# Token preparation of each image inside the last steps of the Mamba pipeline, in place of a block of its own

## The chip, the cores and the metric

One core of a Trainium2 chip runs the whole program in one launch. The metric is the device time of that launch in microseconds (us). All arithmetic is in f32; sort keys and indices are 32-bit integers. TensorE does the matrix products and the 128x128 transposes, VectorE and ScalarE the elementwise work, GpSimd (POOL) additions and the indirect transfers, and SyncE (SP) issues nearly all other transfers. Each engine works through its own queue in program order and waits on semaphores.

## The reference, cut to what matters

x has 16 images of 128 channels and 32x32 = 1024 places.

```
x1  = x + conv_branch(layer_norm_over_channels(x))     # two Mamba layers and a residual path r
t   = x1 as tokens [16, 1024, 128]                     # one token per place
n   = layer_norm(t)                                    # over the 128 channels, eps 1e-5
h   = n @ W_gat                                        # 16 columns: 4 heads x 4 experts
a_src, a_dst = sum over experts of h * att_src, h * att_dst      # 4 + 4 columns
score = graph attention over 524288 edges and 16384 loops (gather h and a_src of each edge's source)
out = t + mixture of 4 experts, top 2 by score, of n   # GELU MLPs, 128 -> 256 -> 128
```

Token preparation is what this document calls the lines from x1 to a_src and a_dst: x1 = v + x (v is the output of the second Mamba layer with its residual, x the input), x1 turned so that tokens lie on the partitions, the norm, the turn back (the experts want channels on the partitions), and the product with the 128x24 matrix [W_gat, W_gat*att_src, W_gat*att_dst], whose 24 columns are one row of the table that the edges gather from. x1, the normalised tokens of all images (64 KB a partition) and the table (16384 rows of 96 bytes) are kept.

## The kernel before, in words

The program is a chain of blocks; all engines meet at the end of each. The first block is the Mamba pipeline with the sort of the edges laid between its instructions. A prologue over 16 images comes first, then a loop of `STEPS` = 82 steps, t = 0 to 81. In step t below `NJ` = 64, TensorE projects one tile of 128 rows of a group of four images (`in_part`, L587), first half of the output (z = 0) and gate (z = 1). ScalarE moves it out and VectorE convolves (`conv`, L930). Nine steps behind (`SCAN_AT`), TensorE gives the step size (`dt_part`, L619), ScalarE makes softplus (`softplus`, L764 to L767, with an activation table load), then the decays of the tile before it (`decay`, L774), then `logarithm` (L781); VectorE adds (`step_size`, L942) and, one step later, scans (`scan`, L952 to L975). Behind a whole group, the output product goes in units of six chunks a step (`out_part`, L604; a chunk is 128 rows of the output weight, 512 KB, loaded by SP into one of four buffers, each load waiting for the chunk that had the buffer). Each step takes them two at a time in three places of TensorE's queue. An image is complete after eight chunks; VectorE norms it (`norm_first`, L981, and `norm_second`, L992 to L1001, in places fixed by dictionaries of steps), ScalarE applies Silu (L807, `put_out`) and in the second layer the result v goes to DRAM (L498). The last scan belongs to step 73, the output chunks of the last four images to steps 74 to 79, their norms and Silu to steps 75 to 80.

The sort's last comparison (L899, L900) is in step 58. Step `search` = 66 begins the search for the places where each partition's part of the edges starts: VectorE counts rows (L1070 to L1074), POOL gathers three sets of 128 rows of 4096 keys (L550, 6 MB), and VectorE compares and sums them at the end of step 68 (L1078, L1081). Two more small steps (lengths by DRAM and back, L527 and L529, and the number of rounds, L1091 to L1098) follow at 69 and 71.

The second block is token preparation. SP loads v and x of an image (L1150), POOL adds them (L1186), SP stores the sum (L1169), TensorE turns it (`turn`, L1196, eight 128x128 transposes), VectorE takes statistics (L1229, L1232), ScalarE the root (L1267), VectorE scale and shift (L1238, L1239), ScalarE normalises (L1272), TensorE turns back (L1216), ScalarE copies to `tok_t` (L1279), TensorE multiplies with the 128x24 matrix (`project`, L1205), VectorE copies the rows (L1247) and SP stores them (L1155). The tiles in PSUM that TensorE writes are double, except the one of the turn back, and each engine runs about an image ahead of the next.

The third block gathers table rows for the edges, 1280 indirect transfers on POOL (L1449), with the experts' products beside them; it needs the whole table. It starts with constants and memsets on POOL (L1419 to L1436), after which VectorE makes the addresses (L1577 to L1580) and POOL fetches the first keys (L1440). A last block mixes.

The order of work on each engine is written out by hand in the loop over t; nothing is planned by costs.

Of the kernel before, what the change touches and what calls it, by code (L numbers as in the profile page):

```python
# [12 lines left out]
P = 128  # L13
# [101 lines left out]
STEPS = KC * (NI - 1) + OUT_AT + (4 * KC - 1) // UNITS + 3  # L115
# [50 lines left out]
def program(nc, a, stop=99):  # L166
# [12 lines left out]
    with ctx:  # L179
# [27 lines left out]
        rounds_i = sb("rounds_i", [1, 1], I32)  # L207

# [19 lines left out]
        with ExitStack() as st, nc.Block() as block:  # L228
            w = [{k: a[f"m{m}_{k}"] for k in ("WinT", "convw", "convb", "WxT", "WdtT", "bdt", "Alog", "D", "WoutT")}
                 for m in (1, 2)]  # L230
            keys = [sb(f"keys{n}", [P, KF], F32, st) for n in range(2)]
            xT = sb("xT", [P, 2, KC, QW], F32, st)
# [36 lines left out]
            len_max = sb("len_max", [1, 1], F32, st)  # L269
            slots_i = sb("slots_i", [1, 1], I32, st)  # L270
# [73 lines left out]
            s_v = first_sem("s_v")  # L344
            s_vst = [first_sem("s_vst0"), first_sem("s_vst1")]
# [17 lines left out]
            search = KC * (NI - 1) + KC + 2  # L363
            spare = keys[1 - keys_in(len(plan))]
            row_of = [xT[:, x].rearrange("p k n -> p (k n)") for x in range(2)] + [spare[:]]
            firsts = w_in[:, 0, 0, :]
            before = w_in[:, 0, 1:4, :]
            len_row = w_in[0:1, 1, 0:3, :]
            len_f = w_in[0:1, 1, 3:5, :]
            pad = w_in[0:1, 0, 4, :].bitcast(I32)  # L370

            @block.sync
            def _(sp):
# [36 lines left out]
                def load_image(b):  # L410
                    if b < B:
                        if b >= 2:
                            sp.wait_ge(s_pt, b - 1)
                        sp.dma_start(xin[b % 2], x_in[b]).then_inc(s_px[b % 2], 16)

# [42 lines left out]
                for t in range(STEPS):  # L458
# [37 lines left out]
                    elif n is not None:  # L496
# [13 lines left out]
                    if t == search - 1:  # L510
# [3 lines left out]
                        sp.wait_ge(s_cmp, done_at[-1])  # L514
                        last = keys[keys_in(len(plan))]
                        sp.dma_start(sorted_d[0:NE, :].rearrange("(p c) o -> p (c o)", p=P),
                                     last[:].bitcast(I32)).then_inc(s_stored, 16)
                        with nc.allow_non_contiguous_dma(reason="one key of a row"):
                            sp.dma_start(first_d[:, :], last[:, 0:1]).then_inc(s_first, 16)
                        sp.wait_ge(s_first, 16)  # L520
                        sp.wait_ge(s_mz, NJ)
                        sp.dma_start(firsts, first_d[:, :].rearrange("p o -> o p").partition_broadcast(P)
                                     .rearrange("p o n -> p (o n)")).then_inc(s_first, 16)
                    if t == search + 3:
                        sp.wait_ge(s_len, 1)
                        with nc.allow_non_contiguous_dma(reason="three places of a row"):
                            sp.dma_start(len_d[:, :].rearrange("o p -> p o"), ends_f[:]).then_inc(s_lend, 16)  # L527
                        sp.wait_ge(s_lend, 16)
                        sp.dma_start(len_row, len_d[:, :].rearrange("(x o) p -> x o p", x=1)).then_inc(s_lend, 16)  # L529
                for x in range(2):  # L530
                    sp.wait_ge(s_vst[x], 16 * B // 2)
                sp.wait_ge(s_lend, 32)

            @block.gpsimd
            def _(g):
# [9 lines left out]
                g.wait_ge(s_mz, NJ)  # L545
# [3 lines left out]
                for x in range(3):  # L549
                    g.indirect_dma_start(row_of[x].bitcast(I32), None,  # L550
                                         sorted_d[0:NE, :].rearrange("(r c) o -> r (c o)", c=KF),
                                         bass.IndirectOffsetOnAxis(ap=row_i[:, x:x + 1], axis=0)).then_inc(s_rows, 16)
                g.wait_ge(s_rows, 48)

            @block.tensor
            def _(t_):
# [81 lines left out]

                t_.wait_ge(s_const, 2)
# [64 lines left out]
            def _(s_):  # L704
# [103 lines left out]

                s_.wait_ge(s_small, 160)
# [1109 lines left out]
```

## Time and profile before

| | us |
|---|---|
| median of 3 runs (lowest, highest) | 4398.14 (4394.29, 4399.58) |
| the profiled execution, its own time | 4400.41 |
| its span | 4398.5 |
| pipeline steps from 65 on, to the end of the last scan | 2080 to 2242.6 |
| output of the last four images | 2242.6 to 2319.1 |
| token block, to the first addresses of the gather block | 2319.1 to 2461.6 |
| gather block | 2461.6 to 4204 |

Over the span TensorE is busy 67%, VectorE 68%, ScalarE 35%, POOL 30%; the mean granted TensorE clock is 0.808 of 2.4 GHz. Times in rows are microseconds from the start of the span. "Idle before" in brackets is how long the engine stood before the instruction and what ended the wait; several instructions of one line are merged into a row, with their number.

### The profile page before, as it was taken

To read this page: it belongs to the slowest core of one execution; us is meant where nothing else is said; L and a number is where in the kernel's file an instruction comes from. 1 tells how busy PE (TensorE), PEld (TensorE's weight loads), DVE (VectorE), ACT (ScalarE), POOL (GpSimd) and SP (SyncE) were. 2 spreads that over 40 slices of the span, in tenths; PEclk is the share of its full clock that TensorE was granted. 3 is DMA by queue.
4 is the path that set the end of the run, shared out by engine and by line. 5 is a ranking of instruction groups with operands and counts; after the bars stand their busy time and mean duration, and the time that the engine had idled before them with its cause. 6 is when DMAs were issued, how large, how long until landed. Compare 5 with 4: busy or idle time off the path is not lost. (4 is left out here: it accounts for less than half of the span.)

```text
span 4398.5 us, 30087 instructions
## 1 busy us (share of the span) xinstructions
PE 2938.8 (67%) x9220; PEld 1502.9 (34%) x9220; DVE 2992.7 (68%) x4591; ACT 1543.2 (35%) x2215; POOL 1333.3 (30%) x1388
## 2 busy tenths in 40 slices
PE   4888899799999998999656334544554553554019
PEld 1333344344444443433226222322222232232019
DVE  6999858787888786986754545654654664565465
ACT  1222225444444454445434123323322322332117
POOL 0000000000000000000002477777777777777600
PEclk8888899899999999999875567766776776777559
DMA  4111322364645454645757311111111111111237
GB/s 144 58 58 53 127 94 81 107 189 131 183 140 177 145 170 144 188 135 177 251 192 219 58 27 49 42 37 44 46 37 44 46 37 37 34 18 17 23 127 287
DMA packets 342679, 458.36 MB, mean 104 GB/s; under 512 B 83156, under 2 KB 257110, under 8 KB 333688
## 3 DMA queue, kind: packets, MB, share of 16 engines
q1 hardware_dynamic: 296760, 416.46, 29.2%
q0 software_dynamic: 45760, 40.00, 5.7%
q8 instruction: 74, 1.21, 0.1%
q14 instruction: 85, 0.70, 0.0%
HBM read 342.80 MB, written 113.51 MB: 104 GB/s over the span
## 5 line engine op out<-in xcount | busy, mean ns | idle before, releaser
L1449 POOL DMA_INDIRECT got<-scratch_tab,src_at x1280 | 1223.1, 956 | 390.1 <-issue 378.5
L587 PE MATMUL in_ps<-xT,w_in 128*128 128x512 f32 x2048 | 936.7, 610 | 4.4 <-issue 4.4
L1396 PE MATMUL hid_ps<-tokens,w 128*128 128x512 f32 x512 | 316.6, 751 | 862.1 <-ACT hid L1615 841.8
L546 POOL MEMSET w_in<- 1x128 int32 x1 | 0.2, 195 | 2064.2 <-PE in_ps L587 2064.2
L587 PEld LDWEIGHTS in_ps<-xT,w_in 128*128 128x128 f32 x2048 | 393.9, 196 | 484.4 <-issue 484.4
L604 PE MATMUL out_ps<-w_out,act 128*128 128x512 f32 x1024 | 472.9, 608 | 68.1 <-issue 35.9
L899 DVE TENSOR_TENSOR keys<-keys 128x1024 f32<-128x1024 f32 x380 | 464.2, 1222 | 10.7 <-ACT keys L713 9.5
L900 DVE TENSOR_TENSOR keys<-keys 128x1024 f32<-128x1024 f32 x380 | 464.0, 1221 | 0.0
L1544 DVE TENSOR_TENSOR hold<-by_value,is_loop 128x256 f32<-128x256 f32 x20 | 8.5, 426 | 631.1 <-ACT by_value L1626 631.1
L1396 PEld LDWEIGHTS hid_ps<-tokens,w 128*128 128x128 f32 x512 | 108.8, 236 | 956.6 <-ACT hid L1615 851.7
L1626 ACT ACTIVATE by_value<-got 128x1536 f32<-128x1536 f32 x20 | 80.6, 4028 | 771.6 <-DMA got<-scratch_tab,src_at 771.6
L604 PEld LDWEIGHTS out_ps<-w_out,act 128*128 128x128 f32 x1024 | 194.6, 194 | 324.4 <-issue 287.6
L930 DVE SCALAR_TENSOR_TENSOR act<-padded,conv_w,act 128x512 f32<-128x512 f32 x192 | 144.1, 750 | 235.7 <-ACT act L744 230.6
L1412 PEld LDWEIGHTS y_ps<-w,hid 128*128 128x128 f32 x2048 | 264.7, 209 | 110.4 <-issue 95.1
L1412 PE MATMUL y_ps<-w,hid 128*128 128x128 f32 x2048 | 290.0, 300 | 0.0
L648 PE MATMUL out_ps<-act,xT 128*128 128x512 f32 x512 | 233.6, 610 | 0.0
L1568 DVE COPY_PREDICATED run<-hop_ps,run 128x1512 f32<-128x1512 int32 (+2 forms) x120 | 202.0, 1683 | 17.8 <-DVE run L1563 0.5
L1615 ACT ACTIVATE hid<-hid_ps,b 128x512 f32<-128x512 f32 x256 | 161.8, 682 | 137.1 <-PE hid_ps L1396 131.9
L1517 DVE TENSOR_TENSOR same<-b_k,hop_ps 128x2048 f32<-128x2048 f32 x84 | 192.1, 2286 | 5.6 <-DVE b_at L1508 0.5
L1518 DVE TENSOR_REDUCE n_same<-same 128x32 f32<-128x2048 f32 x84 | 192.0, 2286 | 2.9
L1407 PE MATMUL y_ps<-b,ident 1*128 1x512 f32 x256 | 161.9, 715 | 0.0
L743 ACT ACTIVATE padded<-in_ps 128x512 f32<-128x512 f32 x64 | 38.3, 598 | 334.4 <-PE in_ps L587 334.4
(267 smaller groups left out, 4078.0 us busy)
## 6 DMA issues: line engine op xcount, KB each, us to landing
w_out<-in_m_WoutT SPq DMA_DIRECT2D x256, 512.0 KB, 4.6
w_in<-in_m_WinT SPq DMA_DIRECT2D x128, 512.0 KB, 4.0
scratch_y<-ys SPq DMA_DIRECT2D x25, 1024.0 KB, 4.0
got<-scratch_tab,src_at POOLq DMA_INDIRECT x1280
xT<-scratch_xt SPq DMA_DIRECT2D x8, 2048.0 KB, 10.0
scratch_sz<-zst SPq DMA_DIRECT2D x64, 256.0 KB, 5.3
gz<-scratch_sz SPq DMA_DIRECT2D x64, 256.0 KB, 5.0
tokens<-scratch_y SPq DMA_DIRECT2D x16, 1024.0 KB, 9.3
```

The source lines that it names most:

```text
L587: last = t_.matmul(in_ps[:, z, :], w_in[:, n % WIN, k, :], xT[:, s % 2, k, :], start=(k == 0), stop=(k == KC - 1))
L604: last = t_.matmul(out_ps[:, 2 * (n % 2) + h], act[:, s % 3, k, i * P:(i + 1) * P], w_out[:, c % WOUT, h * QW:(h + 1) * QW], start=(k == 0 ...
L648: t_.matmul(out_ps[:, 2 + h], xT[:, b // 4 % 2, k, (b % 4) * P:(b % 4 + 1) * P], w_spa[:, k, h * QW:(h + 1) * QW], start=(k == 0), stop=False)
L899: v.tensor_tensor(to_lo, lo, hi, ALU.min).then_inc(s_cmp, 1)
L900: v.tensor_tensor(to_hi, lo, hi, ALU.max).then_inc(s_cmp, 1)
L1396: last = t.matmul(hid_ps[:, f], w1[:, e, f * P:(f + 1) * P], tokens[:, g * QW:(g + 1) * QW], start=True, stop=True)
L1407: t.matmul(y_ps[:, n % 2], ident[0:1, 0:1].to_broadcast([1, P]), b2[:, e, :].unsqueeze(1).to_broadcast([1, QW // P, P]), start=True, stop= ...
L1412: last = t.matmul(y_ps[:, n % 2, c * P:(c + 1) * P], hid[:, n % 2, f, c * P:(c + 1) * P], w2[:, e, f, :], start=False, stop=(c == QW // P ...
L1449: g.indirect_dma_start(got[:, y, t, :], None, tab_d[:, :], bass.IndirectOffsetOnAxis(ap=src_at[:, y, t:t + 1], axis=0))\
L1517: ck(v.tensor_tensor(same[:], key, mark, ALU.is_equal))
L1518: ck(v.tensor_reduce(n_same[:, n:n + part], same[:], AX.X, ALU.add))
L1568: ck(v.copy_predicated(run[:, :, 0:FR - d], hop[:, b, d:FR].unsqueeze(1) .to_broadcast([P, OUTS, FR - d]), run[:, :, d:FR]), wait_apart)
```

## The change

The token block is gone. Its work is done in the first block's loop, from step `TOK_AT` = 66 on, image b in step 66 + b, and the loop has 84 steps. There is one set of PSUM tiles for it: the turn uses `in_ps`, which the input projection no longer needs, and the turn back and the table product share `turn_ps`, half an image at a time. So the turn of an image waits for the normalised tokens of the image before, and each half of the turn back for the copy or rows before it. In SBUF, x1 takes the place of the input weights, v and the normalised tokens lie in a part of `act`, and the token buffer itself (`tok_t`, now outside the blocks) holds the sort's keys and `xT` until they are done. The first 12 images read v from DRAM as before; the last four (`DIRECT` = B − 4) are added where ScalarE leaves them, and their v is not stored. The search for the rows begins in step `SEARCH` = 60 in place of 66, its three row sets are gathered into the two key buffers (the third after the first is summed), compared and summed at the end of steps 62 and 63, and the small steps come at 65 and 66. The addresses of the first keys are made there too, so the gather block can fetch keys before its memsets. The clearing of the first block's semaphores moves from the token block's start to the gather block's end. The diff, cut to its core:

```diff
-STEPS = KC * (NI - 1) + OUT_AT + (4 * KC - 1) // UNITS + 3
+SEARCH = KC * (NI - 1) + 4
+TOK_AT = KC * NI + 2
+DIRECT = B - 4
+STEPS = TOK_AT + B + 2
...
-            keys = [sb(f"keys{n}", [P, KF], F32, st) for n in range(2)]
-            xT = sb("xT", [P, 2, KC, QW], F32, st)
+            keys = [tokens[:, n * KF:(n + 1) * KF] for n in range(2)]
+            xT = tokens[:, 2 * KF:].rearrange("p (x k n) -> p x k n", x=2, k=KC)
...
+            row_of = [last_keys, spare, last_keys]
...
+            xw = [w_in[:, n].rearrange("p k n -> p (k n)") for n in range(3)]
+            xv = [act[:, 2, 2 * n:2 * n + 2].rearrange("p k n -> p (k n)") for n in range(2)]
+            normed = [act[:, 2, 4 + 2 * n:6 + 2 * n].rearrange("p k n -> p (k n)").rearrange("p (k n) -> p k n", n=P)
+                      for n in range(2)]
...
+            tok_ps = in_ps[:].rearrange("p h n -> p (h n)").rearrange("p (k n) -> p k n", n=P)
+            h_ps = turn_ps[:, 0:KC * ROW].rearrange("p (k f) -> p k f", f=ROW)
...
+                def load_tokens(b):
+                    if b < B:
+                        if b >= 3:
+                            sp.wait_ge(s_tt, b - 2)
+                            sp.wait_ge(s_x2[b % 3], 16 * (b // 3))
+                        sp.dma_start(xw[b % 3], x_in[b]).then_inc(s_xw[b % 3], 16)
+                        if b < DIRECT:
+                            if b >= 2:
+                                sp.wait_ge(s_add, b - 1)
+                            sp.wait_ge(s_vst[b % 2], 16 * (b // 2 + 1))
+                            sp.dma_start(xv[b % 2], v_d[b]).then_inc(s_xv[b % 2], 16)
...
-                        if i >= 2:
+                        if i >= DIRECT + 2:
+                            sp.wait_ge(s_add, i - 1)
+                        elif i >= 2:
...
+                    if t >= TOK_AT - 2:
+                        store_x2(t - TOK_AT)
+                        load_tokens(t - TOK_AT + 2)
+                        store_rows(t - TOK_AT - 3)
...
+                    if b < DIRECT:
+                        g.wait_ge(s_xv[b % 2], 16 * (b // 2 + 1))
+                    else:
+                        g.wait_ge(s_v, b + 1)
+                    g.tensor_tensor(xw[b % 3], xv[b % 2] if b < DIRECT else xo[b % 2], xw[b % 3], ALU.add).then_inc(s_add, 1)
...
+                def tokens_turn(b):
+                    if 0 <= b < B:
+                        t_.wait_ge(s_add, b + 1)
+                        if b:
+                            t_.wait_ge(s_norm, b)
+                        else:
+                            t_.wait_ge(s_ez, NJ)
+                        for k in range(KC):
+                            last = t_.transpose(tok_ps[:, k, :], xw[b % 3][:, k * P:(k + 1) * P], ident[:])
+                        last.then_inc(s_tt, 1)
+                def tokens_back(b, half):
+                    if 0 <= b < B:
+                        t_.wait_ge(s_norm, b + 1)
+                        if half:
+                            t_.wait_ge(s_tk, 2 * b + 1)
+                        elif b:
+                            t_.wait_ge(s_row, b)
+                        for k in range(KC // 2):
+                            last = t_.transpose(turn_ps[:, k * P:(k + 1) * P], normed[b % 2][:, half * KC // 2 + k, :],
+                                                ident[:])
+                        last.then_inc(s_bk, 1)
+                def table_part(b):
+                    if 0 <= b < B:
+                        t_.wait_ge(s_tk, 2 * b + 2)
+                        if not b:
+                            t_.wait_ge(s_wt, 1)
+                        for k in range(KC):
+                            last = t_.matmul(h_ps[:, k, :], tok_t[:, b, k * P:(k + 1) * P], w_row, start=True, stop=True)
+                        last.then_inc(s_h, 1)
...
                         in_part(t, 0, 0)
+                    tokens_turn(t - TOK_AT)
                     if t >= SCAN_AT + 1 and t % KC == 2 and t // KC <= NI:
...
                         out_part(c)
+                    tokens_back(t - TOK_AT - 1, 0)
                     if t >= SCAN_AT + 1 and t % KC == 2 and t // KC <= NI:
                         spread(t // KC - 1, 3)
                     else:
@@ -679,6 +803,7 @@
...
                         out_part(c)
+                    tokens_back(t - TOK_AT - 1, 1)
...
                         out_part(c)
+                    table_part(t - TOK_AT - 1)
...
+                def tokens_root(b):
+                    if 0 <= b < B:
+                        s_.wait_ge(s_tst, b + 1)
+                        s_.wait_ge(s_tsh, b)
+                        s_.activation(dev8[:], mv8[:, :, 1], ACT.Sqrt, bias=eps5[:, 0:1]).then_inc(s_tsd, 1)
+                def tokens_normal(b):
+                    if 0 <= b < B:
+                        s_.wait_ge(s_tsh, b + 1)
+                        if b >= 2:
+                            s_.wait_ge(s_bk, 2 * b - 2)
+                        for k in range(KC):
+                            last = s_.activation(normed[b % 2][:, k, :], tok_ps[:, k, :], ACT.Identity,
+                                                 bias=shift8[:, k:k + 1], scale=rstd8[:, k:k + 1])
+                        last.then_inc(s_norm, 1)
+                def tokens_copy(b, half):
+                    if 0 <= b < B:
+                        if not b and not half:
+                            s_.wait_ge(s_rnd, 1)
+                        s_.wait_ge(s_bk, 2 * b + half + 1)
+                        s_.activation(tok_t[:, b, half * QW:(half + 1) * QW], turn_ps[:], ACT.Copy).then_inc(s_tk, 1)
...
                     root((t, 1))
+                    tokens_root(t - TOK_AT)
+                    tokens_copy(t - TOK_AT - 1, 0)
                     turned((t, 4))
                     if t in outs_at and outs_at[t] % 4 == 0:
                         put_out(outs_at[t])
...
+                    tokens_normal(t - TOK_AT)
+                    tokens_copy(t - TOK_AT - 1, 1)
                     if outs_at.get(t, 0) % 4:
                         put_out(outs_at[t])
...
+                def table_rows(b):
+                    if 0 <= b < B:
+                        v.wait_ge(s_h, b + 1)
+                        if b >= 2:
+                            v.wait_ge(s_tab[b % 2], 16 * (b // 2))
+                        v.tensor_copy(rows[:, b % 2], h_ps).then_inc(s_row, 1)
...
+                    table_rows(t - TOK_AT - 2)
+                    tokens_first(t - TOK_AT)
                     scan(t - SCAN_AT - 1)
+                    tokens_second(t - TOK_AT)
...
+                    if t == SEARCH + 2:
+                        v.wait_ge(s_rows, 32)
+                        rows_before(0)
+                        v.sem_inc(s_rowi, 1)
+                        rows_before(1)
+                    if t == SEARCH + 3:
...
+                        rows_before(2)
...
+                load_keys()
+                load_last(0)
                 g.iota(b_node[:], pattern=[[1, BINS]], base=0, channel_multiplier=BINS)
```

The removed token block's code stands above in the kernel before; its statistics, scale and shift, and activations are the same operations on the same shapes, but the copy of the turned-back tokens is made in two halves.

## Rows read from the trace of the kernel before

**Rows 1.** Busy us by stretch: length, engines, PEclk, DMA share, GB/s.

```profile
2080.00:2242.60 162.60, 83.71 (x160) 31.76 (x158) 128.89 (x179) 73.87 (x90) 3.55 (x3) 0.74 0.55 199
...
2242.60:2319.10 76.50, 60.05 (x128) 24.77 (x128) 26.75 (x32) 14.38 (x15) 0.00 (x0) 0.92 0.71 240
...
2319.10:2461.60 142.50, 103.69 (x512) 99.99 (x512) 53.09 (x312) 67.31 (x161) 43.42 (x30) 0.54 0.67 200
```

**Rows 2.** Timeline, step 66: start, duration, engine, line, operation, tiles, idle before.

```profile
2108.25 3.60 PE L604 MATMUL out_ps<-w_out,act 128*128 128x512 f32 x8
...
2111.78 1.12 PE L619 MATMUL dt_ps<-dbl,w_dt 64*128 64x512 f32 x2
...
2108.45 0.60 ACT L787 ACTIVATE bc<-dt_ps 128x512 f32<-128x512 f32 x1 [5.64 <-PE dt_ps L611]
...
2114.22 1.28 ACT L767 ACT_TABLE_LOAD   x1
...
2116.05 1.32 ACT L774 ACTIVATE temps<-temps,rate 128x512 f32<-128x512 f32 x2
...
2117.50 0.06 DVE L957 MEMSET temps<- 128x4 f32 x1 [7.66 <-ACT temps L774]
...
2123.15 0.69 DVE L975 TENSOR_TENSOR act<-temps,gz 128x512 f32<-128x512 f32 x1
```

**Rows 3.** Timeline, steps 67 and 68: TensorE wait, VectorE search.

```profile
2144.79 3.78 PE L604 MATMUL out_ps<-w_out,act 128*128 128x512 f32 x4 [11.37 <-DMA w_out<-in_m_WoutT]
...
2156.34 4.61 DVE L1078 TENSOR_SCALAR xT<-xT,bin_key 128x4096 f32<-128x4096 f32 x2
...
2171.91 4.41 DVE L1081 TENSOR_REDUCE n_in<-keys 128x1 f32<-128x4096 f32 x1
```

**Rows 4.** Timeline, the last four output images and the last Silu.

```profile
2242.67 13.86 PE L604 MATMUL out_ps<-w_out,act 128*128 128x512 f32 x28 [35.91 <-issue]
...
2308.58 1.98 PE L604 MATMUL out_ps<-w_out,act 128*128 128x512 f32 x4 [0.68 <-DMA w_out<-in_m_WoutT]
...
2318.00 1.06 ACT L807 ACTIVATE area<-area 128x1024 f32<-128x1024 f32 x1 [4.15 <-DVE area L1001]
```

**Rows 5.** Timeline of VectorE in step 63.

```profile
2056.29 2.33 DVE L930 SCALAR_TENSOR_TENSOR act<-padded,conv_w,act 128x512 f32<-128x512 f32 x3 [5.24 <-ACT act L744]
...
2064.05 0.06 DVE L957 MEMSET temps<- 128x4 f32 x1 [4.11 <-ACT temps L774]
```

**Rows 6.** Timeline of the token block, parts of one image.

```profile
2401.47 1.95 PE L1196 MATMUL tok_ps<-ident,x 128*128 128x128 f32 x8
...
2403.45 1.68 DVE L1229 BATCH_NORM_STATS2 st<-tok_ps 128x6 f32<-128x128 f32 x8 [1.41 <-PE tok_ps L1196]
...
2404.91 3.45 PE L1205 MATMUL h_banks<-w_row,tokens 128*128 128x24 f32 x16
...
2406.46 0.20 DVE L1238 RECIPROCAL scale<-std 128x8 f32<-128x8 f32 x1 [0.65 <-DVE mean L1232]
...
2406.90 2.91 ACT L1272 ACTIVATE normed<-tok_ps,bias,scale 128x128 f32<-128x128 f32 x8 [0.53 <-DVE bias L1239]
...
2409.71 2.35 POOL L1186 TENSOR_TENSOR x<-x_v,x_raw 128x1024 f32<-128x1024 f32 x1 [5.48 <-DMA x_raw<-in_x]
```

**Rows 7.** Timeline of TensorE early in the token block.

```profile
2358.67 1.86 PE L1205 MATMUL h_banks<-w_row,tokens 128*128 128x24 f32 x16
...
2360.38 1.07 PE L1196 MATMUL tok_ps<-ident,x 128*128 128x128 f32 x8
```

**Rows 8.** Timeline, token block end and gather block start.

```profile
2452.12 0.36 DVE L1247 COPY rows<-h_banks 128x192 f32<-128x192 f32 x1 [3.06 <-PE h_banks L1205]
...
2455.34 0.20 POOL L1419 IOTA back<- 128x64 f32 x1 [23.28 <-POOLq L1124]
...
2462.04 0.98 POOL L1440 DMA_INDIRECT edge_k<-scratch_sorted,key_at  x1 [0.84 <-DVE key_at L1580]
...
2477.84 0.94 POOL L1449 DMA_INDIRECT got<-scratch_tab,src_at  x1 [0.30 <-issue]
```

More of the change, by code:

```diff
@@ L344, in program @@
             s_v = first_sem("s_v")
+            s_xv = [first_sem("s_xv0"), first_sem("s_xv1")]
+            s_xw = [first_sem(f"s_xw{n}") for n in range(3)]
+            s_x2 = [first_sem(f"s_x2{n}") for n in range(3)]
+            s_add = first_sem("s_add")
+            s_tt = first_sem("s_tt")
+            s_tw = first_sem("s_tw")
+            s_wt = first_sem("s_wt")
+            s_tch = first_sem("s_tch")
+            s_tst = first_sem("s_tst")
+            s_tsd = first_sem("s_tsd")
+            s_tsh = first_sem("s_tsh")
+            s_norm = first_sem("s_norm")
+            s_bk = first_sem("s_bk")
+            s_tk = first_sem("s_tk")
+            s_h = first_sem("s_h")
+            s_row = first_sem("s_row")
+            s_tab = [first_sem("s_tab0"), first_sem("s_tab1")]
+            s_rnd = first_sem("s_rnd")
             s_vst = [first_sem("s_vst0"), first_sem("s_vst1")]
@@ L495, in _ @@
                             load_ln(1)
-                    elif n is not None:
+                    elif n is not None and n < B + DIRECT:
                         sp.wait_ge(s_v, n - B + 1)
@@ L509, in _ @@
                         load_out(c + WOUT)
-                    if t == search - 1:
+                    if t == SEARCH - 1:
+                        sp.wait_ge(s_cmp, done_at[-1])
+                        with nc.allow_non_contiguous_dma(reason="one key of a row"):
+                            sp.dma_start(first_d[:, :], last_keys[:, 0:1]).then_inc(s_first, 16)
+                        sp.dma_start(sorted_d[0:NE, :].rearrange("(p c) o -> p (c o)", p=P),
+                                     last_keys.bitcast(I32)).then_inc(s_stored, 16)
                         sp.wait_ge(s_const, 3)
@@ L513, in _ @@
                                      pad).then_inc(s_stored, 16)
[L514 to L519, printed above, removed]
+                    if t == SEARCH:
                         sp.wait_ge(s_first, 16)
-                        sp.wait_ge(s_mz, NJ)
                         sp.dma_start(firsts, first_d[:, :].rearrange("p o -> o p").partition_broadcast(P)
                                      .rearrange("p o n -> p (o n)")).then_inc(s_first, 16)
-                    if t == search + 3:
+                    if t == SEARCH + 5:
                         sp.wait_ge(s_len, 1)
@@ L1002, in norm_second, with rows_before, tokens_first, tokens_second @@
                         v.wait_ge(s_rs, n - B + 1)
+                def rows_before(y):
+                    ck(v.tensor_scalar(row_of[y], row_of[y], bounds[:, y:y + 1], None, ALU.is_lt))
+                    ck(v.tensor_reduce(n_in[:, y:y + 1], row_of[y], AX.X, ALU.add))
+                def tokens_first(b):
+                    if 0 <= b < B:
+                        v.wait_ge(s_tt, b + 1)
+                        for k in range(KC):
+                            op = v.bn_stats(stats8[:, k, :], tok_ps[:, k, :])
+                        kt(op)
+                        v.wait_ge(s_norm, b)
+                        for k in range(KC):
+                            op = v.bn_aggr(mv8[:, k, :], stats8[:, k, :])
+                        op.then_inc(s_tst, 1)
+                def tokens_second(b):
+                    if 0 <= b < B:
+                        v.wait_ge(s_tst, b + 1)
+                        v.wait_ge(s_tsd, b + 1)
+                        kt(v.reciprocal(rstd8[:], dev8[:]))
+                        v.scalar_tensor_tensor(out=shift8[:], in0=mv8[:, :, 0], scalar=-1.0, in1=rstd8[:],
+                                               op0=ALU.mult, op1=ALU.mult).then_inc(s_tsh, 1)
+                def table_rows(b):
+                    if 0 <= b < B:
+                        v.wait_ge(s_h, b + 1)
+                        if b >= 2:
+                            v.wait_ge(s_tab[b % 2], 16 * (b // 2))
+                        v.tensor_copy(rows[:, b % 2], h_ps).then_inc(s_row, 1)
                 def norms(place):
```

298 lines of the change are left out of this document (84 added, 214 removed).

## The prediction

> **What bounds the kernel now.** Read the stretches first [rows 1]. The Mamba pipeline's last steps (66 to 73, with neither input projection nor sort) lie in the first one, its last four output images in the second, the token block in the third. TensorE is 51% busy in the first, 78% in the second, 73% in the third, and the DMA engines stand at 0.55, 0.71 and 0.67: the third stretch looks like work that could be laid into the holes of the first. It is 142.5 us, and nothing of the edge stage runs in it: block 3 waits for the whole table. So one expects much; the queues say otherwise.
>
> Read next who waits for whom in one step of that first stretch [rows 2]. In step 66 TensorE's step-size product (L619) ends at 2112.90, ScalarE needs until 2117.37 for softplus, a table load and the decays (4.47), VectorE waited 7.66 us and then scans from 2117.50 to 2123.84. Step by step this is a serial loop of ScalarE and VectorE, and TensorE stays out of it only because its product is ready ahead of time. That freedom is what the change spends.
>
> Step 68 is different [rows 3]: the search in the sorted rows holds VectorE from 2156.34 to 2176.3, 20.0 us, and TensorE waited 11.37 us for output weights while 6 MB of rows were gathered.
>
> **What is removed.** The token block: the next block's first instruction comes at 2455.34, the last two-chunk set of output products ends at 2310.56 [rows 4]. Also the 20.0 us of step 68.
>
> **What is added, part by part.**
>
> The search moves to steps 60, 62 and 63, where TensorE bounds and VectorE waits. Of two rows' work (2 × 6.7 us; a row is a third of 20.0) after step 62, the 5.24 us wait ahead of the convolution at 2056.29 is the cover that I take in full [rows 5]: 13.4 − 5.2 = 8.2 late. ScalarE's decay covers another 4.1 of it, the third row (7) and its bookkeeping (0.7) have no cover: 8.2 − 4.1 + 7.7 = 11.8 us late at the scan that feeds step 65. If nothing covered it, 21; if the gathers (now 4 MB beside 0.6 of the DMA engines) also starve TensorE in step 61, up to 11.4 more, the stall seen in step 67. I take 11.8.
>
> Step 66 has the first image. Its end 2123.84 becomes 2135.6; tokens_second (0.44, from the reciprocal's start 2406.46 to the activations' 2406.90) and the eight normalising activations (2.91) follow [rows 6], that is 2138.9, and about 1 for handovers and first use: TensorE's turn of image 1, which waits for them (s_norm), begins step 67 at 2140.
>
> Steps 67 to 72. Follow the queues. tokens_turn(b) is first in TensorE's step and waits for tokens_normal(b−1), at the end of ScalarE's last step. Behind it are two output chunks, half a back turn, then the step-size product. So that product is no longer ahead: ScalarE's softplus waits for it, decay stands behind softplus, the scan behind decay, tokens_second behind the scan, tokens_normal behind that, the second half copy behind it, and table_part, last in TensorE's step, waits for this copy. One period is the sum of the chain:
>
> turn 1.07 (fast) to 1.95 (slow) [rows 6, 7]; two chunks 3.60 [rows 2] to 5.58 (one of them slow, 3.78 [rows 3]); half a back turn 0.6 to 1.0 (half of a turn); L619 1.12; ScalarE 4.47; scan 6.34; second 0.44; normal 2.91; half copy 0.60 (the same 128x512 copy as L787); table 1.86 to 3.45; eight handovers 0.3. That is 23.3 with TensorE at 2.4 GHz and 28.2 at 1.2 GHz. Between them TensorE idles about 5 us in mid step (for the first half copy, behind decay, logarithm, root), so the clock falls in part of each: I take 25.5. Six periods are 153 (140 to 169). Hidden in it: bn_stats and bn_aggr (2.3), the norms (5.4), Silu (2.3), row copies.
>
> Step 73 has no softplus: turn 1.5, tokens_first 2.3, scan with its head 7.8, second 0.4, normal 2.9, copy 0.6, table 2.6, handovers 0.4: 18.5 (16 to 20).
>
> Steps 74 to 78, image weights streaming. TensorE: turn 1.07 to 1.95, six chunks 10.8 (one pair slow: 12.8), back 1.1 to 2.0, table 1.86 to 3.45: 14.8 to 20.2. Before, 128 records in the 67.9 us from 2242.67 to 2310.56 are 12.7 us for six chunks, 1.9 above 10.8, waits for weights. DMA work: the second stretch spends 76.5 × 0.71 = 54 us of full engines on its bytes (18.4 MB: 2.96 us/MB), 10.9 for a step's 3.7 MB; the token block 142.5 × 0.67 / 16 = 6.0 per image. Sum 16.9 while v is still loaded, 15.4 later. Neither end goes under 15.4 by much; I take 18.0 (15.5 to 21). Five are 90, and 1.9 in step 75, where VectorE's norm_first stands ahead of the row copy that the back turn waits for: 92.
>
> The end, from step 79's turn. Two chunks 6.0; ScalarE's copy, normal, copy, Silu, with the table loads of 1.28, and the root for image 31 end at 15.0; norm_second to 20.4 (5.4 of the 7.4 us from the last product's end to Silu at 2318.00, norm_first and its root being the rest [rows 4]); tokens_first(14), root, copy, normal, copy to 27.6, Silu of image 31 at 30.0; the add 2.35 [rows 6], turn, statistics, root and second to 37.7; normal and copies to 41.4; table of image 14 to 44.9; back turn and copies of image 15 to 48.8; table 52.2, row copy 52.7 and 2.9 to the next block, as from 2452.12 + 0.36 to 2455.34 [rows 8]: 55.5 (51 to 60). TensorE is taken slow here, as it was in the token block from 2366 on.
>
> The gather block: the keys are fetched ahead of the memsets, the fetch comes 0.6 us into the block and not at 2462.04 (6.7 in): 6.1 less before the first gather at 2477.84 [rows 8]. It bounds the stage behind it from there, so it counts in full. A page's rule would raise the period: the Trainium skill, "ScalarE: Activation LUTs", section "What ACT_TABLE_LOAD costs", puts a switch at 1.28 us and a drain of 1.38 behind it. In this trace softplus's load ends at 2115.50 and its Exp is over, and the decays begun, by 2116.05 [rows 2]: 0.55 us hold no such drain. By the page the six periods would be 8 us longer and the result slightly slower. The row is taken.
>
> **The sum.** 2140 + 153 + 18.5 + 92 + 55.5 = 2459.0 for the next block's start, against 2455.3: +3.7; minus 6.1: −2.4. The profiled execution took 4400.4 (span 4398.5), which gives 4398.0; the median of the runs shown is 2.3 lower than that execution, so 4396. The 142.5 us block goes, and comes back as longer steps: step 79 began at about 2307 without the images and will begin at 2403.5.
>
> Ends: all fast, 2137 + 140 + 16 + 77.5 + 51 = 2421.5, −34 −6 = −40; all slow with the stall of step 61, 2151 + 169 + 20 + 107 + 60 = 2507, +52 −6 = +46. All terms at one end together is unlikely.
>
> **Rivals.**
> A. TensorE stays at 2.4 GHz through the steps. For it: the table in 1.86 and the turn in 1.07 at 2358 to 2361 [rows 7], and a step has 10.8 us of dense chunks. Against: the 5 us idle in each. Period 23.8, steps 74 to 78 at 16, the end 53: −10 −10 −2.5 gives 4373.
> B. Slower: TensorE's short transposes, table products and the mid-step wait leave it at 1.2 GHz in each step, and image weights wait behind token loads. For it: the token block at granted clock 0.54 although busy 73%, and a chunk of 3.78 for 1.80 after a wait. Period 27.7, steps at 20: +13 +10 gives 4419. It decides once the eleven steps are 1.0 us each over the forecast's.
> C. The serial loop isn't there, because the queues overlap more than I read: the images lie in the holes of steps 67 to 73 (their TensorE work of 5 to 7.5 us; the first stretch has 162.6 − 83.7 = 79 us idle, 10 a step) and only steps 74 to 79 and the end are paid. Then 4396 − 6 × 11 = 4330. Against it are the waits in program order.
> D. The moved search starves TensorE as in step 67: the forecast and 11 more, 4407, or with B more.
>
> **Chances.** Forecast 0.33 (own range 4384 to 4408), A 0.25, B 0.25, C 0.07, D 0.10. A measurement of this kernel tells 0.2% (8.8 us) from no change. Faster: A and C nearly whole, a fifth of the forecast: 0.37. Slower: B, half of D, a little of the forecast: 0.33. The same: 0.30. The range for 8 in 10 leaves out C and the far end of B: 4365 to 4434.
>
> **What would show it.** In the changed kernel's timeline L619's products in steps 67 to 72 come 23 to 28 us apart, each some 7 us behind a turn, and ScalarE's softplus waits for TensorE, not for the scan. The searches of step 62 and 63 hold VectorE 20 us. The last turn of 16 starts near 2436, the first indirect fetch of the gather block is within 1 us of its start, and the first gather near 2475. The block order and the gather stage itself  keep their length. Periods of 14 to 17 us in steps 67 to 72 would prove C, and the forecast wrong in its main term; a gather stage of another length would make all of this beside the point.

## The result, and the profile after

| | before | after |
|---|---|---|
| median of 5 and 5 runs (lowest, highest) | 4398.14 (4394.29, 4401.42) | 4416.59 (4414.61, 4420.59) |
| ratio | | 1.0042, 95% interval [1.0029, 1.0055] |
| the profiled execution: own time, span | 4400.41, 4398.5 | 4419.19, 4416.7 |
| next block's first instruction | 2455.34 | 2477.44 |
| first key fetch | 2462.04 | 2478.19 |
| first gather of table rows | 2477.84 | 2493.65 |

Slower by 18.5 us, where no change (4396) was forecast. From the first gather on the two executions need 1920.7 and 1923.1 us: 15.8 of the 18.2 us between the spans lie ahead of it.

Stretches of the changed kernel, which answer to [rows 1] (the first is as long; the second holds steps 71 to 74, the third steps 75 to 79, the last what follows from step 80's turn on):

```profile
2080.00:2242.30 162.30, 105.52 (x293) 49.76 (x292) 106.44 (x231) 82.17 (x128) 14.78 (x6) 0.80 0.58 180
2242.30:2339.70 97.40, 45.24 (x167) 30.30 (x166) 47.16 (x123) 42.17 (x72) 9.73 (x4) 0.61 0.40 133
2339.70:2437.80 98.10, 71.92 (x267) 41.20 (x266) 36.96 (x124) 33.14 (x68) 11.72 (x5) 0.88 0.67 222
2437.80:2477.40 39.60, 21.05 (x88) 18.03 (x88) 11.10 (x44) 13.17 (x27) 2.34 (x1) 0.50 0.16 39
```

The holes of the first stretch are smaller (TensorE 105.5 us busy for 83.7), but the second has new ones: TensorE is 46% busy, its granted clock 0.61, the DMA engines 0.40 busy.

Timeline of step 72 in the changed kernel, as [rows 2] and [rows 6] of before. L735 turns an image, L747 turns half of one back, L758 is the table product, L706 the step-size product, L1192 VectorE's copy of the table's rows:

```profile
2270.57 3.61 PE L758 MATMUL turn_ps<-zst,tokens 128*128 128x24 f32 x16 [6.61 <-ACT tokens L959]
...
2274.00 1.95 PE L735 MATMUL in_ps<-ident,w_in 128*128 128x128 f32 x8
...
2279.88 0.36 DVE L1192 COPY zst<-turn_ps 128x192 f32<-128x192 f32 x1
...
2280.39 1.09 PE L747 MATMUL turn_ps<-ident,act 128*128 128x128 f32 x4 [4.44 <-DVE zst L1192]
...
2281.40 2.07 PE L706 MATMUL dt_ps<-dbl,w_dt 64*128 64x512 f32 x2
...
2283.51 0.69 ACT L890 ACTIVATE temps<-dt_ps,dt_b 128x512 f32<-128x512 f32 x1 [9.02 <-PE dt_ps L706]
...
2288.08 0.06 DVE L1113 MEMSET temps<- 128x4 f32 x1 [3.47 <-ACT temps L900]
...
2294.77 2.90 ACT L949 ACTIVATE act<-in_ps,shift,rstd 128x128 f32<-128x128 f32 x8 [2.78 <-DVE shift L1183]
2297.52 0.63 ACT L959 ACTIVATE tokens<-turn_ps 128x512 f32<-128x512 f32 x1
...
2298.21 3.61 PE L758 MATMUL turn_ps<-zst,tokens 128*128 128x24 f32 x16 [5.00 <-ACT tokens L959]
...
2301.65 1.73 PE L735 MATMUL in_ps<-ident,w_in 128*128 128x128 f32 x7
```

This is the serial loop that the prediction read out of the queues: turn, step-size product, softplus (which waited 9.02 us for TensorE), scan, shift, normal, copy, table, next turn: 27.65 us from 2274.00 to 2301.65.

But there is one more wait, in the row copy. VectorE's copies (images 7, 8 and 10) and SP's issues of the stores of images 5, 6 and 8 (L474; ahead of the first of them weights, L426, and the x1 store, L468), in the changed kernel:

```profile
2349.27 0.36 DVE L1192 COPY zst<-turn_ps 128x192 f32<-128x192 f32 x1 [3.52 <-DMA scratch_tab<-zst]
2370.02 0.36 DVE L1192 COPY zst<-turn_ps 128x192 f32<-128x192 f32 x1 [12.05 <-DMA scratch_tab<-zst]
...
2409.17 0.36 DVE L1192 COPY zst<-turn_ps 128x192 f32<-128x192 f32 x1 [8.04 <-DMA scratch_tab<-zst]
```

```profile
2336.45 2.04 SPq L426 DMA_DIRECT2D w_out<-in_m_WoutT  x2
2338.54 0.43 SPq L468 DMA_DIRECT2D scratch_x<-w_in  x1
...
2339.98 1.07 SPq L474 DMA_DIRECT2D scratch_tab<-zst  x1
2361.54 1.33 SPq L474 DMA_DIRECT2D scratch_tab<-zst  x1
...
2401.15 0.70 SPq L474 DMA_DIRECT2D scratch_tab<-zst  x1
```

Image 5's rows were copied at 2301.86 and stored only at 2339.98, last in SyncE's step, behind that step's output weights, the x1 store and both token loads. There are two row buffers, so image 7's copy waited for that store. What each engine waited for from 2100 to 2480, in the changed kernel (sum in us, times, longest):

```profile
DVE zst L1192 <- DMA scratch_tab<-zst: 51.3, 7, 12.1
...
ACT temps L890 <- PE dt_ps L706: 60.6, 7, 13.8
...
PE turn_ps L747 <- ACT tokens L959: 45.9, 11, 8.7
PE turn_ps L747 <- DVE zst L1192: 37.4, 11, 5.6
```

The head of the gather block, as [rows 8]: the fetch comes 0.75 us into the block, and the first gather 16.2 after the block's start, for 22.5 before.

```profile
2477.44 0.19 POOL L1443 IOTA back<- 128x64 f32 x1 [23.39 <-POOLq L236]
...
2478.19 0.97 POOL L1453 DMA_INDIRECT edge_k<-scratch_sorted,key_at  x1 [0.32 <-issue]
...
2493.65 0.94 POOL L1462 DMA_INDIRECT got<-scratch_tab,src_at  x1 [0.30 <-issue]
```

### The profile page after: what moved, and what is told of

It is laid out like the page before. It is cut to its first block and busy times, and to the rows that moved or that the text cites. A ratio compares the mean times of both kernels' runs of the same rounds, so it can differ in the third digit from the quotient of the medians.

```text
span 4416.7 us, 30154 instructions
## 1 busy us (share of the span) xinstructions
PE 2930.2 (66%) x9220; PEld 1485.5 (34%) x9220; DVE 2996.5 (68%) x4591; ACT 1551.9 (35%) x2237; POOL 1336.5 (30%) x1388
## 5 line engine op out<-in xcount | busy, mean ns | idle before, releaser
L674 PE MATMUL in_ps<-tokens,w_in 128*128 128x512 f32 x2048 | 936.8, 610 | 5.8 <-issue 5.8
L674 PEld LDWEIGHTS in_ps<-tokens,w_in 128*128 128x128 f32 x2048 | 394.1, 196 | 484.4 <-issue 484.4
L1055 DVE TENSOR_TENSOR tokens<-tokens 128x1024 f32<-128x1024 f32 x380 | 464.5, 1222 | 10.8 <-ACT tokens L839 9.7
L1056 DVE TENSOR_TENSOR tokens<-tokens 128x1024 f32<-128x1024 f32 x380 | 464.3, 1222 | 0.0
L770 PE MATMUL out_ps<-act,tokens 128*128 128x512 f32 x512 | 234.8, 613 | 0.0
```

Of the source, the lines that this page charges most:

```text
L674: last = t_.matmul(in_ps[:, z, :], w_in[:, n % WIN, k, :], xT[:, s % 2, k, :], start=(k == 0), stop=(k == KC - 1))
L770: t_.matmul(out_ps[:, 2 + h], xT[:, b // 4 % 2, k, (b % 4) * P:(b % 4 + 1) * P], w_spa[:, k, h * QW:(h + 1) * QW], start=(k == 0), stop=False)
L1055: v.tensor_tensor(to_lo, lo, hi, ALU.min).then_inc(s_cmp, 1)
L1056: v.tensor_tensor(to_hi, lo, hi, ALU.max).then_inc(s_cmp, 1)
```

## The experiments

The starts of L735's turns give each kernel's periods. "Six" is from step 67's turn to step 73's, "five" from step 74's to step 79's. "Store wait" is VectorE's wait for the row store in 2150 to 2480.

| kernel | ratio to before, 95% | step 67 | six | five | first gather | store wait |
|---|---|---|---|---|---|---|
| before | 1 | | | | 2477.8 | |
| changed | 1.0042 [1.0029, 1.0055] | 2142.5 | 159.1 | 97.9 | 2493.7 | 51.3 |
| e1 row store first | 0.9952 [0.9938, 0.9965] | 2140.5 | 148.5 | 74.7 | 2454.8 | 0 |
| f8 four row buffers | 0.9957 [0.9943, 0.9970] | 2144.1 | 148.4 | 74.9 | 2458.8 | 0 |
| f5 row store ahead of token transfers | 0.9957 [0.9943, 0.9972] | 2138.7 | 149.2 | 80.3 | 2460.5 | 21.3 |
| f4 row store on ScalarE's queue | 0.9972 [0.9954, 0.9990] | 2140.6 | 148.4 | 81.5 | 2466.0 | 21.2 |
| e2 step-size product first | 1.0006 [0.9997, 1.0015] | 2139.7 | 144.5 | 98.9 | 2477.5 | 56.8 |
| e3 = e1 + e2 | 0.9940 [0.9926, 0.9953] | 2140.5 | 139.0 | 77.0 | 2447.4 | 0 |
| f6 = e1 + copy first | 0.9934 [0.9913, 0.9955] | 2137.2 | 143.2 | 76.2 | 2443.6 | 0 |
| f2 = e3 + copy first | 0.9892 [0.9877, 0.9907] | 2140.4 | 121.7 | 75.5 | 2425.4 | 0 |
| f1 = e3 + shift first | 0.9902 [0.9886, 0.9917] | 2139.1 | 132.2 | 74.8 | 2430.3 | 0 |
| f3 = e3 + both | 0.9891 [0.9876, 0.9906] | 2135.1 | 130.1 | 77.5 | 2426.1 | 0 |
| e4 search alone, on before | 0.9974 [0.9963, 0.9986] | | | | 2462.2 | |
| f0 keys alone, on before | 0.9986 [0.9977, 0.9995] | | | | 2470.7 | |

f4, f5 and f6 ran on another chip (last section), where all takes longer, so their ratios compare among themselves and only roughly with the rest, and the ranges in us of their expectations can't be read off their times. From the first gather to the end of the span the profiled executions of the rest differ by up to 8 us (1920.5 in f1, 1928.3 in f3), though no edit lies there: the first gather is the sharper measure.

### Row store first (e1)

```
 for t in range(STEPS):
+    store_rows(t - TOK_AT - 3)
     load_in(2 * t + 3)
...
         load_tokens(t - TOK_AT + 2)
-        store_rows(t - TOK_AT - 3)
```

> One edit of the changed kernel: SP stores the table rows of an image at the start of its step and no longer at its end behind the stores and loads of x1, x and v. Theory R (the row buffer): in steps 70 to 79 TensorE's first half back turn waits for VectorE's row copy, which waits for the store of two images before, issued last in the step and landing 7 us (median) later; in steps 67 to 78 those waits of TensorE are 33 us, and after each the next pair of chunks takes 4.5 to 5.8 us and not 3.6. All of it goes: 25 to 45 us less than 4416.6, that is 4372 to 4392, and the row copy waits for no transfer in those steps. Rival D (load): the rows of 96 bytes land late wherever they are issued because the DMA engines are full, or weights come late in their place: 0 to 10 us less, 4407 to 4417.

37.3 us came back, 4379.27 (4376.47 to 4380.23), in Theory R's range and below the kernel before; Rival D is out. The two stretches, first of the changed kernel, then of this one:

```profile
2142.54:2301.65 159.11, 94.92 (x309) 52.29 (x309) 95.85 (x223) 86.03 (x136) 16.08 (x7) 0.76 0.54 179
2322.98:2420.85 97.87, 78.81 (x281) 43.88 (x282) 34.75 (x119) 29.34 (x64) 9.37 (x4) 0.90 0.69 231
```

```profile
2140.51:2289.05 148.54, 91.96 (x308) 51.88 (x309) 98.55 (x226) 86.02 (x136) 15.82 (x7) 0.76 0.59 193
2310.39:2385.14 74.75, 71.10 (x281) 40.86 (x282) 38.08 (x119) 29.24 (x64) 9.40 (x4) 0.98 0.87 304
```

10.6 of the 38.9 us by which the first gather moves come from the six periods, 23.1 from steps 74 to 78. These now run at 95% of TensorE, clock 0.98, and DMA share 0.87: 15.0 a step, the packed steps that rival A forecast at 16. TensorE's own wait for the row copy (L747) fell by less than that, from 37.4 to 11.3 us between 2100 and 2480. The rest is in the main pace: in steps 75 to 78 of the changed kernel TensorE waits 5.60, 5.30, 4.08 and 4.08 us for the copy, and the two chunks behind take 4.65, 4.52, 5.24 and 5.30 us where they take 3.60 elsewhere in these steps, while the granted clock of steps 74 to 78 is 0.90, here 0.98. Step 75 of the changed kernel, and the same place of this one:

```profile
2349.78 1.08 PE L747 MATMUL turn_ps<-ident,act 128*128 128x128 f32 x4 [5.60 <-DVE zst L1192]
2350.65 4.65 PE L691 MATMUL out_ps<-w_out,act 128*128 128x512 f32 x8
```

```profile
2332.22 0.63 PE L747 MATMUL turn_ps<-ident,act 128*128 128x128 f32 x4 [2.12 <-DVE zst L1192]
2332.69 3.60 PE L691 MATMUL out_ps<-w_out,act 128*128 128x512 f32 x8
```

### Four row buffers (f8)

Moving the store also moves it past loads. This leaves it in place and takes away what makes VectorE wait.

```
-rows = zst[:, 0, 0:2 * KC * ROW]...          # two buffers
+rows = [padded[n // 2][:]... for n in range(4)]   # the convolution's tiles, free by then
...
-if b >= 2: v.wait_ge(s_tab[b % 2], 16 * (b // 2))
+if b >= 4: v.wait_ge(s_tab[b % 4], 16 * (b // 4))
```

> The changed kernel with its row stores left where they are (end of SyncE's step, behind the token transfers) and four buffers for rows, in the convolution's padded tiles that are free by then, instead of two in zst: VectorE's row copy waits for the store of image b-4, not of b-2. Theory A (the wait for the store, 51.3 us in 7 times, is the cost, and the store's place mattered only through it): the wait is gone and most of the 37.3 us of the moved store come without moving it, 0.993 to 0.997 of before, first gather at 2453 to 2463. Rival B (the store's place matters otherwise too, through the order of the loads that it goes ahead of, and the waits of VectorE only hid another): 1.000 to 1.004 of before, first gather at 2475 or later, with a new wait of TensorE or VectorE in place of this one.

Theory A holds. The periods are e1's to 0.2 us. The store is no quicker (6.8 us to land in the median of all sixteen, as in the changed kernel) and still issued 10.6 to 16.8 us behind the turn of its step (steps 74 to 78; 16.2 to 21.9 in the changed kernel). It is only waited for by nobody:

```profile
L475 SPq DMA_DIRECT2D scratch_tab<-padded x16: 359/580/1393, 2216.1 to 2439.4; - x16
...
who waited for it (us, times):
...
DMA to landing us min/median/max: 2.3/6.8/9.4
```

So the wait is shown as the cause, apart from the store's place.

### Why the store is late (f5, f4)

f5: the store stays at the end of SyncE's step, ahead of `store_x2` and `load_tokens`. f4: ScalarE issues it at the end of its own step (images 0 to 14), on its own queue.

> The changed kernel with the row store still at the end of SyncE's step, but ahead of the x2 store and the two token loads. Theory A: it no longer stands behind their waits and bytes, only behind the weights; 60 to 100 percent of what the move to the head of the step gave (37.3 us): 4379 to 4394 us. Rival B (the place in the step is what counts, as SyncE reaches its end only when the next turn's buffers come free): under 10 us gained, 4407 to 4417 us.

> The changed kernel with the row stores of images 0 to 14 issued by ScalarE at the end of its step, on ScalarE's queue, instead of by SyncE at the end of its step behind the token transfers; nothing else. Theory A (the store is late because it is issued late, in SyncE's order behind the waits and the three transfers of the token work): it is issued when ScalarE gets there, about the time at which VectorE has copied the rows, so VectorE's wait for it (51.3 us in 7 times) falls below 15 us and the time to 4375 to 4392 us. Rival B (the transfers share the sixteen DMA engines, and a store issued beside them lands no sooner whatever its queue): landing stays at 7 us or more and the wait above 35 us, 4405 to 4417 us.

Both more than halve the wait (51.3 us). f5 gives back 33.2 of the 38.9 us that e1 gives at the first gather, as its Theory A had it; f4 gives back 27.7. For f4 and for f5, stores and their landing:

```profile
L1026 ACTq DMA_DIRECT2D scratch_tab<-zst x15: 366/367/595, 2207.3 to 2442.4; - x15
...
who waited for it (us, times):
  DVE zst L1197: 21.2, 3
...
DMA to landing us min/median/max: 2.3/3.4/13.0
```

```profile
L474 SPq DMA_DIRECT2D scratch_tab<-zst x16: 360/433/978, 2209.9 to 2441.4; - x16
...
  DVE zst L1192: 21.3, 5
...
DMA to landing us min/median/max: 2.3/5.4/8.6
```

Rival B of f4 (the engines are shared, so no queue helps) falls: the landing is 3.4 us in the median, for 6.8 in the changed kernel (7.9 for the twelve stores up to 2440). But e1's stores land in 7.4, later than the changed kernel's, and cost nothing. When the store is issued counts more than how fast it lands. f5 issues its stores 11.0 to 15.2 us behind the step's turn, about as f8 does; how much of its gain is issue and how much landing isn't separated. The expectation for f4's wait (under 15) missed.

### Step-size product first (e2, e3)

```
 for t in range(STEPS):
...
+    if t > TOK_AT:
+        dt_part(t - SCAN_AT)
     tokens_turn(t - TOK_AT)
```

> One edit of the changed kernel: in steps 67 to 72 TensorE's step-size product stands ahead of the token turn and not behind the turn, two chunks and a half back turn. Theory L (the serial loop of the prediction): ScalarE's softplus waits for that product 9 to 14 us a step; with it gone the loop is softplus to decay 4.5, scan 6.3, second 0.4, normal 2.9, half copy 0.6, table 1.9, turn 1.1: the period falls from 26.5 us (mean of six) to 18 to 21, 30 to 45 us less, or 20 to 35 if the row waits, left as they are, grow in the shorter steps: 4377 to 4397. Rival S: TensorE's own work and the row wait set the period, the product's place is worth only the 5 to 8 us of one step: 4408 to 4417.

> Both edits, rows stored at the start of the step and the step-size product ahead of the turn. Theory R and L together: 60 to 85 us less than 4416.6, 4332 to 4357, periods near 18 us in steps 67 to 78. If either theory is wrong the sum is that of the other edit alone. If both waits overlap (they hide one another) the sum is 30 to 45 us.

e2 came in at 4402.57, between its theories: L's periods of 18 to 21 us are 24.1, and S's 5 to 8 us are too few. Softplus's wait fell from 60.6 to 20.4 us, but the six periods only from 159.1 to 144.5, and the wait for the store grew to 56.8. e3, 4372.34, is 44.3 us below the changed kernel, the case of overlapping waits (30 to 45), not the sum of two. e3's step 72 shows what held the loop instead:

```profile
2261.27 0.36 DVE L1194 COPY zst<-turn_ps 128x192 f32<-128x192 f32 x1
...
2272.65 2.90 ACT L951 ACTIVATE act<-in_ps,shift,rstd 128x128 f32<-128x128 f32 x8 [6.57 <-DVE shift L1185]
2275.39 0.64 ACT L961 ACTIVATE tokens<-turn_ps 128x512 f32<-128x512 f32 x1
...
2276.08 3.61 PE L758 MATMUL turn_ps<-zst,tokens 128*128 128x24 f32 x16 [8.77 <-ACT tokens L961]
...
2279.52 1.73 PE L735 MATMUL in_ps<-ident,w_in 128*128 128x128 f32 x7
```

The second half copy of image b−1 needs nothing of image b, yet it stands behind `tokens_normal(b)`, which waits for the shift behind the scan; the table waits for the copy.

### What holds the loop (f2, f1, f3, f6)

Copy first: `tokens_copy(b − 1, 1)` ahead of `tokens_normal(b)` on ScalarE. Shift first: `tokens_second` ahead of `scan` on VectorE, with `tokens_root` ahead of softplus.

> The version with both reorderings (row store at the head of SP's step, dt_part ahead of the turn), and in it the token work's VectorE second part (reciprocal and shift) ahead of the scan, with its ScalarE root behind evacuate instead of behind the logarithm. Theory A (what sets the period now is the chain turn, statistics, scan, shift, normal, copy, table, next turn): normal's wait for shift (47.0 us in 9 times) and half or more of TensorE's wait for the copy (52.9 us in 11) go, the steps 74 to 78 fall from 14.3-16.6 to 11-13, the first gather comes 15 to 35 us earlier: 4337 to 4357 us. Rival B (TensorE's own work with clock and transfers is the bound of steps 67 to 73, and the early root holds ScalarE behind the statistics, so softplus comes late): those steps stay at 22 to 24 and the tail gains 3 a step at most: 4360 to 4375 us. Rival C (softplus late makes VectorE late): slower than 4375 us.

> The version with both reorderings, and in it ScalarE's second half copy of the image before ahead of normal(b) instead of behind it, so that TensorE's table no longer stands behind normal's wait for VectorE's shift. Theory A: TensorE's wait for the copy (52.9 us in 11 times) falls below 20, but the next turn then waits for normal(b), so 3 to 15 us are gained: 4357 to 4369 us. Rival B (next turn needs normal anyway, and table only changes places with the wait): 4369 to 4375 us, nothing gained. Rival C: normal 2.2 us later each step, slower by 5 to 20 us.

> Both of these orders at once (shift ahead of the scan, root behind evacuate, second half copy ahead of normal). Theory A: as the first, and the table's wait all but gone: 4330 to 4355 us. Rival B: within 4 us of the first alone, as there normal no longer waits and the copy behind it costs 2.9 us a step at most.

> The changed kernel with the row store at the head of SyncE's step and the second half copy ahead of normal, dt_part left where the change has it. Against the row store alone at 4379.3 us (in another comparison, 0.9952 of before) and the version with all three edits at 0.9892. Theory A (dt_part behind the turn costs on its own, softplus waits 45.6 us there): this lands between, 0.991 to 0.9935 of before. Rival B (with the copy early the turn no longer waits long, so dt_part behind it comes soon enough): equal to all three within 0.1 percent, 0.988 to 0.990.

f2, two lines exchanged, moves the first gather 22.0 us ahead of e3's (0.9892 of before for 0.9940), more than its theory allowed (4352.4 for 4357 to 4369). The table's wait for the copy fell from 52.9 to 4.8 us, and the next turn's wait for normal rose only from 9.6 to 30.5. Its step 72: the table is done before normal begins.

```profile
2253.13 3.61 PE L758 MATMUL turn_ps<-zst,tokens 128*128 128x24 f32 x16 [0.69 <-ACT tokens L961]
...
2259.00 2.90 ACT L951 ACTIVATE act<-in_ps,shift,rstd 128x128 f32<-128x128 f32 x8 [5.92 <-DVE shift L1185]
...
2262.05 1.94 PE L735 MATMUL in_ps<-ident,w_in 128*128 128x128 f32 x8 [5.30 <-ACT act L951]
```

f1 came in at 4356.24, in Theory A's range, though not as it said: normal's wait went, but ScalarE's early root now waits 113.0 us for the statistics (52.9 in e3), and steps 74 to 78 stayed at 15.0, where 11 to 13 had been forecast: TensorE is busy 71.5 of their 74.8 us. f3 (4353.87) adds nothing to f2; both of its theories allowed that time. f6's 0.9934 lies in its Theory A's range, at the edge and with an interval wider than that range; its periods say more. Without the early step-size product it has 143.2 for f2's 121.7: that edit is worth 18 us in the first gather (2443.6 to 2425.4), but only once the copy is out of its way (7 from e1 to e3). The edits act on links of one loop, and each pays when the next isn't late already.

### The two other parts, alone (e4, f0)

> The kernel before with one part of the change alone: the search for the rows at steps 60 to 66, with its three row sets in the two key buffers, the token block left as a block. Prediction's terms: 20.0 us go from step 68 and the wait for output weights of step 67 (11.4 us) with them, 11.8 us come in steps 62 to 63: 8 to 20 us less than before, 4378 to 4390. Rival: what step 68 loses was hidden under other waits, and the 11.8 remain: 4400 to 4410.

> The kernel before with the early key fetch alone: bases computed and gathers' keys and positions copied before the last block, so that the first key fetch waits for no VectorE copy of its own there. My step: 6.1 us earlier gather, 4390 to 4394 us. Rival (the fetch's start is set by GpSimd's iota and descriptors, which stay): within 2 us of before, 4396 to 4400 us.

e4: 4386.68, 11.7 us less than before; the last four images' products begin at 2227.10 and not at 2242.67 [rows 4], the token block 15.4 earlier, and the first gather 15.6 us earlier. That is within its theory's 8 to 20. f0: the first gather is 7.1 us earlier, the ratio makes it 6.2 us, for 6.1 forecast.

## Why the prediction was wrong

By its own steps, predicted and measured:

| term | predicted | changed | e1 |
|---|---|---|---|
| turn of step 67 | 2140 | 2142.5 | 2140.5 |
| six periods | 153 | 159.1 | 148.5 |
| step 73 | 18.5 | 21.3 | 21.3 |
| steps 74 to 78 | 92 | 97.9 | 74.7 |
| from step 79's turn | 55.5 | 56.6 | 53.4 |
| block start to first gather | 16.4 | 16.2 | 16.2 |

**The step that failed is "Hidden in it: [...] row copies".** The copy's 0.36 us were hidden, and its wait was not in the sum. The prediction followed TensorE, ScalarE and VectorE through the step and named each queue's order, but not SyncE's: the row store is last there, behind the step's weights, and behind a store and two loads of 512 KB that wait for this step's adds and turns. Before, the store was issued 0.4 us after the copy (2355.9 after 2355.55) and landed in 3.0 us; one row of [rows 8] shows no wait for a store, and it was taken to stay so. e1 and f8, two ways round the same wait, bring the first gather 38.9 and 34.9 us forward, f8's step 67 being 1.6 us later than the changed kernel's.

**Two errors partly cancelled.** Without the wait, steps 74 to 78 take 74.7 us and not 92. Their 18.0 each was a middle between a fast 14.8 and a slow 20.2; the granted clock in e1 is 0.98 there, the fast end (1.07 for the turn), and DMA 0.87. Had the store been seen, 4396 would still have come out some 17 us too high for that kernel: rival A's terms (23.8, 16) were near e1's (24.8, 15.0), and its 4373 near 4379. So it was luck that the forecast missed by only 20.6 us, and that 4416.6 lies within 4365 to 4434: the upper half of that range was made from a slow clock and a starved step 61, not from this wait. Step 73 was too short by 2.8 us with or without the wait (21.3 us in both): its second scan instruction took 3.30 us and not the 1.20 of steps 69 to 72, and the table product 3.61 for the 2.6 taken.

**What held.** The loop and its links (L735 in periods of 22.5 to 31.7 us, softplus waiting for TensorE), step 67's start, the end, and the key fetch (6.1, measured 6.2 alone). ScalarE's table switch stayed at 1.28 us with the next activation behind it at once, as taken (in step 72 from 2284.79 to 2286.07, the activation at 2286.09). Rival C (images in the holes) is refuted, 26.5 us a period. Rival D too: where 11 us were feared, in step 61 of the changed kernel, TensorE waited 0.60 us, its only wait for weights between 1990 and 2080:

```profile
2022.77 1.98 PE L691 MATMUL out_ps<-w_out,act 128*128 128x512 f32 x4 [0.60 <-DMA w_out<-in_m_WoutT]
```

Rival B reached the measured time (4419 for 4416.6) on a wrong mechanism. The clock was not at 1.2 GHz in each step (granted 0.76 of 2.4 GHz in the six periods, 0.90 in steps 74 to 78), and from 2100 to 2480 TensorE waited for no weights. With the row wait gone the six periods keep their 0.76 and steps 74 to 78 rise to 0.98, so what the clock lacked there was the wait's effect.

**The search.** It was booked as 20.0 us off step 68 and 11.8 us late in steps 62 and 63, inside the step sum, so 8.2 us gained. Alone it gains about 11.5 us (0.9974). The first gather moves by 15.6 us, but in the profiled execution what follows it took 1925.7 us and not 1920.7, inside the spread named above. With it and the keys (6.2) taken out, moving the token work itself cost about 36 us in the changed kernel, and with f2's three edits gains about 30. That the parts add up was not tried.

Open: that the steps 74 to 78 of f2 are bound by TensorE with DMA close behind (71.7 of 75.5 us busy, DMA 0.87) is read from the stretch; no run took either away.

## What to carry to other kernels

When work is moved into a pipeline's step, follow the buffers that it fills to the instruction that empties them, and that instruction through its own queue: here a store of 96 KB, last in SyncE's step, cost 37 us, and either an earlier issue or two more buffers took them back. Within the step, put what depends only on the image before (copy, table) ahead of what depends on this one (normal); one exchanged pair of lines moved the first gather by 22 us. With the store first, the step-size product first and the copy first, the same move of the token work runs in 4352.43 us (4351.56 to 4352.98), 1.1% below the kernel before.

## What the runs showed of the hardware

- The same store of 96 KB landed in a median of 3.0 us in the token block before, 6.8 on SyncE's queue behind token transfers (changed, all sixteen; 7.9 for the twelve up to 2440), 5.4 ahead of them (f5), 3.4 on ScalarE's queue with the same transfers running (f4), with one of 13.0.
- After TensorE waits of 4.08 to 5.60 us (changed kernel, steps 75 to 78), two output chunks took 4.52 to 5.30 us and not 3.60; after one of 2.12 us (e1, step 75) they took 3.60.
- One chip ran every kernel some 15% longer (before 5057.63 us, 5048.4 to 5082.84). The steps up to the first gather take as long as on the others (f4's step 67 at 2140.6, its six periods 148.4 us, as in e1 and f8); the gathers, from first to last, took 2282 us for 1685, with an unchanged 0.944 us for each of the 1280 instructions. Why that chip's gather block is slower stays open.
